# Attention in a transformer block: mask and row maximum of each head in one VectorE operation, exponentials released four heads at a time

## The reference

```python
h = tok_ref(x, pos_table, nest_table, seg_table, W)
h = h + attn_ref(layernorm(h), wq, bq, wk, bk, wv, bv, wo, bo)
h = h + ffn_ref(layernorm(h), router_w, router_b, fc1_w, ...)      # top-2 of 8 experts

def attn_ref(inputs_q, ...):            # 8 heads of 64, S = 128
    q, k, v = (einsum('bsd,dhk->bshk', inputs_q, w) + b for w, b in ...)
    logits = einsum('bqhd,bkhd->bhqk', q / sqrt(64), k)
    logits = where(mask, logits, -1e10)   # one block of 128: causal
    weights = softmax(logits, axis=-1)
    x = einsum('bhqk,bkhd->bqhd', weights, v)
    return einsum('bqhd,hdf->bqf', x, wo) + bo
```

## Time and profile before

| | us |
|---|---|
| median of 3 runs | 1486.12 (1485.44 to 1490.86) |
| the profiled execution, its time | 1479.45 |
| the profiled execution, span of the trace | 1477.7 |
| attention stage (to about 1010 us of the span) | about 1010 |
| busy: PE / DVE / ACT / POOL | 1300.5 / 1195.4 / 1057.6 / 889.5 |

### The profile page before, as it was taken

The page is one execution under the profiler, slowest core; times in us unless marked ns, Lnnn a source line. Parts: engine busy times, 40 slices in busy tenths (PEclk is TensorE's granted clock), DMA queues, the critical chain, the costliest instruction groups (busy, mean ns, idle before and its releaser), DMA issues.

```text
span 1477.7 us, 42129 instructions
## 1 busy us (share of the span) xinstructions
PE 1300.5 (88%) x11234; PEld 1128.5 (76%) x11235; DVE 1195.4 (81%) x3683; ACT 1057.6 (72%) x3382; POOL 889.5 (60%) x1161
## 2 busy tenths in 40 slices
PE   1699999999999999999999999993399999699996
PEld 0488777777777777777777777773399999699996
DVE  4478888888888888888888888884588888588885
ACT  0599888888888888888888888882255555355553
POOL 3134566656665666566656665666366767477775
PEclk9999999999999999999999999996699999899998
DMA  4042111101110111011101110111789999899995
GB/s 150 3 175 79 33 46 39 40 31 45 38 40 31 45 38 40 31 45 38 40 31 45 38 40 31 45 38 57 248 306 343 345 337 340 278 335 346 338 348 187
DMA packets 91501, 188.43 MB, mean 128 GB/s; under 512 B 18404, under 2 KB 38588, under 8 KB 90812
## 3 DMA queue, kind: packets, MB, share of 16 engines
q1 hardware_dynamic: 50748, 66.35, 14.7%
q10 hardware_dynamic: 20864, 76.87, 13.6%
q0 software_dynamic: 19840, 44.62, 8.6%
HBM read 50.40 MB, written 57.44 MB: 73 GB/s over the span
## 4 chain that ended last, share of the span: by engine, by line
PE 33%; DVE 19%; issue 16%; ACT 12%; DMA 10%; POOL 6%; SPq 2%; DVEq 1%; ACTq 0%; POOLq 0%
ACT probs L640 6%; PE ps L1137 6%; PE ps L1147 4%; PE ps L1050 3%; DMA v<-xs 3%; ACT v L627 3%; PE ps L1052 3%; PE ps L1051 3%; DVE neg_max L813 3%; PE ps L1202 3%; DVE masked L809 3%; DVE probsT L817 2%; ACT qT L618 2%; PE ps L1164 2%; PE ps L1120 2%
## 5 line engine op out<-in xcount | busy, mean ns | idle before, releaser
L640 ACT ACTIVATE probs<-masked,neg_max 128x128 f32<-128x128 f32 x1024 | 398.5, 393 | 9.9 <-DVE neg_max L813 8.0
L529 POOL DMA_INDIRECT xs<-normed,row x256 | 266.1, 1039 | 79.7 <-issue 72.4
L497 POOL TENSOR_TENSOR probs<-probs,inv_sums 128x512 f32<-128x512 f32 x128 | 133.0, 1039 | 268.0 <-DVE inv_sums L821 267.9
L640 ACT ACTIVATION_READ_ACCUMULATOR probs<-masked,neg_max 128x1 f32 x1024 | 193.8, 189 | 0.0
L809 DVE TENSOR_TENSOR masked<-ps,causal 128x1024 f32<-128x1024 f32 x128 | 155.7, 1216 | 37.7 <-PE ps L1113 36.1
L1050 PE MATMUL ps<-xT_hi,w_now 128*128 128x256 f32 x576 | 178.8, 310 | 6.8 <-issue 6.1
L1137 PE MATMUL ps<-probsT,v 128*64 128x128 f32 x2048 | 140.2, 277 | 35.2 <-DVE probsT L817 35.2
L594 ACT ACTIVATE masked<-ps,w_now 128x256 f32<-128x256 f32 x288 | 120.7, 470 | 65.0 <-PE ps L1052 55.1
L1051 PE MATMUL ps<-xT_lo,w_now 128*128 128x256 f32 x576 | 163.3, 283 | 0.0
L1052 PE MATMUL ps<-xT_hi,w_now 128*128 128x256 f32 x576 | 163.2, 283 | 0.0
L986 DVE SCALAR_TENSOR_TENSOR probsT<-ps,w_now,masked 128x256 f32<-128x256 f32 x288 | 126.1, 480 | 41.7 <-PE ps L1052 21.6
(11 more groups left out here) (190 smaller groups left out, 3264.9 us busy)
## 6 DMA issues: line engine op xcount, KB each, us to landing
w_now<-w_parts ACTq DMA_DIRECT2D x144, 514.0 KB
v<-xs SPq DMA_DIRECT2D x108, 260.0 KB
kT<-xs SPq DMA_DIRECT2D x36, 260.0 KB
normed<-h SPq DMA_DIRECT2D x32, 256.0 KB, 2.6
pads<-pad_rows SPq DMA_DIRECT2D x8, 520.0 KB, 2.8
xs<-pad_rows SPq DMA_DIRECT2D x8, 520.0 KB, 3.6
xs<-normed,row POOLq DMA_INDIRECT x256, 2.4
xs<-pads SPq DMA_DIRECT2D x12, 260.0 KB
```

The source lines that it names most:

```text
L529: pool.indirect_dma_start((xs[0], xs_parts)[k], bass.IndirectOffsetOnAxis(ap=row[par][:, k, j:j + 1].bitcast(U32), axis=0), normed2[par][: ...
L640: ins = nc.scalar.activation(probs[par][:, n], masked[par][:, n], ACT.Exp, bias=neg_max[par][:, n:n + 1], scale=1.0, accum_out=sums[par][: ...
```

## The change

Mask and maximum become one VectorE operation per head, `tensor_tensor_reduce` of 128x128: it adds `causal` (now 0 or -3e38) to the scores, multiplies by -1, writes the negated masked scores to `masked`, and keeps the running minimum, which is the negated maximum. ACT undoes the sign with `scale=-1.0`. The step `scores` does four heads, the step `max` the other four, and each ends with an increment of `max_ready`; both halves of `exp` wait for their own.

```diff
-            link(pool.memset(causal[:], HUGE))
-            link(pool.affine_select(out=causal[:], in_=causal[:], compare_op=ALU.is_ge, fill=NEG_INF, base=0,
+            link(pool.memset(causal[:], 0.0))
+            link(pool.affine_select(out=causal[:], in_=causal[:], compare_op=ALU.is_ge, fill=-HUGE, base=0,
                                     pattern=[[-1, 128]], channel_multiplier=1))
...
                     b, par, half = OB * o + i, i % 2, st[2]
+                    act.wait_ge(max_ready, LEAD + 2 * b + half + 1)
                     if half == 0:
-                        act.wait_ge(max_ready, LEAD + b + 1)
 
                         act.wait_ge(pTb_full, LEAD + b - 1)
                     for n in range(half * PAIRS, (half + 1) * PAIRS):
                         ins = nc.scalar.activation(probs[par][:, n], masked[par][:, n], ACT.Exp, bias=neg_max[par][:, n:n + 1],
-                                                   scale=1.0, accum_out=sums[par][:, n:n + 1])
+                                                   scale=-1.0, accum_out=sums[par][:, n:n + 1])
...
+            def mask_max(par, first):
+
+                carry_wait(dve)
+                for n in range(first, first + PAIRS):
+                    ins = V.tensor_tensor_reduce(masked[par][:, n], ps[:, SCORES + n // PAIRS, (n % PAIRS) * S:(n % PAIRS + 1) * S], causal[:],
+                                                 -1.0, 3.4e38, ALU.add, ALU.min, neg_max[par][:, n:n + 1])
+                return ins
...
                 elif kind == "scores":
                     dve.wait_ge(scores_full, LEAD + b + 1)
                     dve.wait_ge(probs_ready, LEAD + b - 1)
-                    V.tensor_tensor(masked[par][:], ps[:, SCORES:SCORES + 2].rearrange("p a (n k) -> p (a n) k", n=4),
-                                    causal[:].unsqueeze(1).broadcast_to([S, HEADS, S]), ALU.min).then_inc(masked_ready, 1)
+                    mask_max(par, 0).then_inc(max_ready, 1)
                 elif kind == "max":
-                    dve.wait_ge(masked_ready, LEAD + b + 1)
-                    V.tensor_reduce(neg_max[par][:], masked[par][:], AX, ALU.max, negate=True).then_inc(max_ready, 1)
+                    mask_max(par, PAIRS).then_inc(max_ready, 1)
...
-                    pe.wait_ge(masked_ready, LEAD + b)
+                    pe.wait_ge(max_ready, LEAD + 2 * b)
                     cols = slice(j * S, (j + 1) * S)
```

More of the change, by code:

```diff
@@ L35 @@
 WBUFS = 4
-NEG_INF = -10000000000.0
 HUGE = 3.0e38
@@ L266, in build @@
         qk_full = led_sem("qk_full"); qk_ready = led_sem("qk_ready"); v_full = led_sem("v_full"); v_ready = led_sem("v_ready")
-        scores_full = led_sem("scores_full"); masked_ready = led_sem("masked_ready"); max_ready = led_sem("max_ready")
+        scores_full = led_sem("scores_full"); max_ready = led_sem("max_ready")
         probs_ready = led_sem("probs_ready"); pTa_full = led_sem("pTa_full"); pTb_full = led_sem("pTb_full")
```

## The result

The changed kernel takes 1530.62 us (median of 4 runs, 1529.42 to 1531.86), the kernel before 1487.19 beside it: a ratio of 1.0289, 95% interval 1.0266 to 1.0311. The change makes the kernel 43 us slower. The prediction had 1484.5 and a range up to 1510.

What follows compares the result with a forecast made beforehand. PE was taken to bound the attention stage (busy 884 of 930 us), VectorE counting only at n=3 and n=0. Terms summed to -0.05 us per group, times 32 groups -1.6 us: 1486.1 to 1484.5 us, range 1476 to 1510.

Steps and rivals of the forecast that it cites:

- The change, part by part: VectorE's mask and maximum, 2.27 us per sequence, give way to eight pairs, 2.20 us; sum -0.05 us per group.
- four rivals: Pair of 0.30 to 0.36 us (0.28), half-rate pair 0.43 (0.08), pair 0.26 (0.12), early exponentials on the path (0.05).
- rival 1: VectorE's fused operation plus accumulator read costs 0.30 to 0.36 us; at 0.34, +23 us, 1509; chance 0.28.
- three signs of being wrong: Fused operations 0.30 us or more apart, fused operations stretched beside POOL, or waits appearing in n=1 and n=2.
- The pair: One fused VectorE operation plus its accumulator read: 0.275 us, at least 0.26; four are 1.10, eight 2.20.
- Where VectorE's time counts: Only before PE's `mix` waits for the copy: 0.35 us at n=3, 0.85 at n=0 per group, 35.2 in all.
- second four of `n = 0`: Four pairs replacing the maximum in n=0: 1.10 against 1.13 us, -0.03 us per group.
- first four of `n = 3`: Four pairs and increment replacing the mask in n=3: +0.01 us per group; a gain worth nothing, a loss counting in full.
- POOL's cover of the first four in `n = 0`: L826 ends after POOL's `residual` anyway, covering 0.88 us of delay: 0 per group, +0.11 without the cover.
- The increment: VectorE's semaphore increment before each four: 0.05 us for `scores`, nothing for `max`; about 0.15 where VectorE really waited.
- The early exponentials: ACT's first four exponentials start some 2 us earlier; ACT's 8.0 us of waits for `neg_max` go, gaining nothing.
- rival 4: ACT's early exponentials are on the path: -8.0 us of waits and the -1.6, 1476.5 us; chance 0.05.

Runs made afterwards that it cites:

- a_shift20: Changed kernel with 20 bare increments at the head of VectorE's program: 1471.05 us, ratio 0.9880 to the kernel before; 1.0092 on the fifth chip.
- a_shift64: Changed kernel with 64 bare increments at the head of VectorE's program: ratio 1.0138 to the kernel before.
- a_03: Changed kernel with fused operations only in n=3 and n=0, loop kept, body 308 instructions: ratio 1.0396 to the kernel before.
- b_body64: Kernel before with eight extra increments behind each mask, loop body 307 instructions, no fused operation: ratio 0.9989 to the kernel before.

## Why the prediction was wrong

**The step that failed** is in "The change, part by part": it priced what comes ("eight pairs, of the operation and the read of its accumulator") by the time on the engine alone, and the sum had no term for the number of instructions in the loop and the place where it begins. That term was put at nothing without a reason; it measured 59.6 us (1530.62 against 1471.05 with the loop moved). "Two instructions of VectorE became sixteen" makes a body of 364 in place of 243, and where the loop happened to begin, that reaches into a fourth block. None of the four rivals named it, so the range could not hold the result; rival 1, the dear pair, had the right sign for a wrong reason. And none of its three signs of being wrong came: the pairs are not 0.30 us apart, they are not stretched beside POOL, and no waits appear in `n = 1` and `n = 2`. The trace of before could not show the stall, but the number of instructions could be counted.

The size of the missing term can be worked out from the rows. From one stalled turn to the next PE's matmuls L1130 are 63.28 us apart (614.42 to 677.70), and without the stall a turn is 58.37 (559.89 to 618.26, L1144 of `n = 0` in a_shift20). Four parts nearly make up the 4.91 us between them: the 2.75 of idle time at the end; half of the 4.78 us in which PE was busy at a clock of 0.50, that is 2.39; 0.29 x 1.80 = 0.52 at 0.71; less the 0.59 us that `mix` of this `n = 0` no longer waits. Their sum is 5.07. This turn is one of the longer ones: from the first stalled turn to the thirteenth it is 751.45 us, 62.62 for each.

```profile
238.75 1.12 PE L1130 MATMUL ps<-ident,probs 128*128 128x128 f32 x4 [2.84 <-DVE probs L831]
...
677.70 0.66 PE L1130 MATMUL ps<-ident,probs 128*128 128x128 f32 x4 [2.75 <-DVE probs L831]
...
990.20 1.11 PE L1130 MATMUL ps<-ident,probs 128*128 128x128 f32 x4 [3.04 <-DVE probs L831]
```

```profile
559.89 1.09 PE L1144 MATMUL ps<-probsT,v 128*64 128x128 f32 x16 [0.59 <-DVE probsT L824]
...
618.26 1.09 PE L1144 MATMUL ps<-probsT,v 128*64 128x128 f32 x16 [0.59 <-DVE probsT L824]
```

13 times the mean difference of 4.25 is 55 us; the medians of the changed kernel and of a_shift20 are 59.6 apart (on two chips on which the kernel before takes the same to 0.6 us). a_shift64 stalls as often, but has no second stop at the multiply (it starts at 601.43, straight after the reciprocal, where the changed kernel had 1.04 us), and PE waits 1.66 us in place of 2.60:

```profile
602.17 0.83 PE L1132 MATMUL ps<-ident,probs 128*128 128x128 f32 x4 [1.66 <-DVE probs L833]
```

So the price of a stall depends on the place too: here 36.8 us in all (1507.87 against 1471.05).

**The pair** was taken as 0.275 us and bounded below by 0.26, since "that the read costs nothing is excluded by ACT's 0.09". It is 0.21: the engine starts the next fused operation together with the read. ScalarE's row was no bound for VectorE. By the figures of the Trainium skill, VectorE: DVE Perf Modes, section The TRN2 errata, the pair was an estimated 0.32; the measured 0.21 does not agree with it.

**Where VectorE's time counts** was right, and what it is worth was not. Without the stall, PE waits for the copy at `n = 0` alone, 0.59 us in place of 0.85, and no longer at `n = 3`:

```profile
PE ps L1144 <- DVE probsT L824: 17.6, 32, 0.9
```

That is 17.6 us less than the 35.2 of before, and the medians say that the kernel gains 16.7 (1487.79 to 1471.05). That these two agree is in part luck. In the two traces the attention stage ends only 8.9 us earlier, by the last projection on PE:

```profile
1011.19 1.14 PE L1147 MATMUL ps<-w_o,mixedT 128*128 128x128 f32 x8
```

```profile
1002.27 1.14 PE L1154 MATMUL ps<-w_o,mixedT 128*128 128x128 f32 x8
```

The spans are nearly the same (1477.7 and 1478.7 us). The expert stage, which the change does not touch, is 9.9 us longer in a_shift20. The traces are from two chips, and the profiled execution of a_shift20 is the slowest of its six (1480.74 us). So half of the gain of the medians is not accounted for by the traces. With the measured pair the prediction's own places give: second four of `n = 0`, 0.84 against 1.13 (616.00 to 616.84), -0.29; `n = 3`, both fours together more than its whole wait of 0.35; 0.64 us per group or -20 us. So the mechanism held, and the term was mis-sized: -1.6 us predicted, -16.7 measured in the medians. One step in it was wrong as well: a gain in the first four of `n = 3` "would be worth nothing", since L826 would then stand behind POOL. In a_shift20 that multiply (now L833) starts at 608.16, 0.14 us before POOL's ends (607.27 + 1.03), and takes its usual 0.69 us:

```profile
607.27 1.03 POOL L496 TENSOR_TENSOR probs<-probs,inv_sums 128x512 f32<-128x512 f32 x1 [1.25 <-DVE inv_sums L828]
...
608.16 0.69 DVE L833 TENSOR_TENSOR probs<-probs,inv_sums 128x512 f32<-128x512 f32 x1
```

**POOL's cover of the first four in `n = 0`** was right: the time saved there is lost again. In a_shift20 the multiply is stretched even more than in the earlier trace rows, and ends 0.55 us after `residual` (614.26 + 1.81 against 614.24 + 1.28):

```profile
614.26 1.81 DVE L833 TENSOR_TENSOR probs<-probs,inv_sums 128x512 f32<-128x512 f32 x1
616.00 0.28 DVE L778 CUSTOM_DVE_ANT_0 masked<-ps,causal 128x128 f32<-128x128 f32 x1
```

```profile
614.24 1.28 POOL L503 TENSOR_TENSOR residual<-h,bias_o 128x512 f32<-128x512 f32 x1
```

**The increment** costs 0.11 us in `n = 3` (pitch in front of the first pair 0.17, 606.94 to 607.11 in a_shift20, against 0.06, 611.85 to 611.91, in the kernel before), where 0.05 was taken. It is inside the room that the cheap pair leaves.

```profile
606.94 0.15 DVE L828 RECIPROCAL inv_sums<-sums 128x4 f32<-128x4 f32 x1
607.11 0.29 DVE L778 CUSTOM_DVE_ANT_0 masked<-ps,causal 128x128 f32<-128x128 f32 x1
```

**The early exponentials** were valued at nothing, and measured so on the second and fifth chips. On a chip of the first kind this was not tried. There the attention stage is 8.9 us shorter while PE's waits for the copy alone fell by 17.6, which leaves no room for rival 4's further 8 us.

## What to carry to other kernels

When a change multiplies small instructions inside a loop, count the loop body's instructions and where it begins as well as their time; look at the instruction queue's packets and for "issue" in front of the first operation of each turn. If a loop stalls there, try a few empty instructions ahead of it or write the loop out before giving the change up: on chips where the kernel before takes 1487 us, 20 of them turned +2.9% into -1.2%. And repeat a gain of 1% on a second chip: here it turned into a loss of 0.9% on another.

## What was not expected of the hardware

- A taken branch of VectorE costs nothing while the loop touches at most three blocks of 128 instructions, and about 3 us, 2.91 and 3.05 in the rows, once it touches four (twelve programs agree). A second stop of 1.0 to 2.0 us follows where the next border is 4 or 12 instructions away. Where the borders lie was inferred from a_03 and b_body64 and met four predictions; the block length is an estimate from packets and from this table.
- PE's granted clock fell to 0.50 after 2.60 us of waiting at such a place, and what that cost (2.39 + 0.52 us) was more than the wait itself.
- The read of a fused operation's accumulator overlaps the next fused operation completely on VectorE.
- Straight code is not free either: written out, the changed kernel has VectorE wait for "issue" before the copy, 15.9 us in 18 waits (a_unroll2), and the kernel before, written out too (b_unroll), 1.0 us in one. Whether this is the fetching was not separated.
